# Moving the operands of TensorE's products to 0 or 64 bytes modulo 128 in a fused four-layer graph kernel

## The chip, the core and the metric

The program runs on one core of one Trainium2 chip. The metric is the device time of one execution in microseconds (us). Engines are named as in the profile: PE is TensorE's matmul side, PEld its weight loads, DVE is VectorE, ACT is ScalarE, POOL is GpSimd, SP is SyncE, which issues all transfers.

## What is computed

The input is 32 graphs of 256 nodes with 256 features, `x`, and a 256 x 256 matrix `adj` for each. Four blocks follow one another, each with a residual and a layer norm:

```
x = layernorm(x + relu(concat(x, adj @ x / deg) @ W.T))
x = layernorm(x + GCN(x, adj))                # three layers, two with relu and bias
x = layernorm(x + attention(x, adj))          # 8 heads of 64: softmax(q k^T) mixed with adj and exp(-adj)
x = layernorm(x + softmax_n(sum_m(q k^T * adj)) * v)
```

## The kernel before

**Split products.** Most products are made from two parts of each operand: a high part in the type fp32r and a low part, the rest, also fp32r. `product` (L1515 and on) issues high x high, high x low and low x high into the same PSUM bank. ACT makes the high part while it copies (`copy`, L409), DVE the low part by a subtraction (`lo`, L881). The tiles with the names `..._h` and `..._l` hold them: the weights `w0`, `w123`, `wqkv`, `wout`, `w3`; the adjacency `adjT` (four graphs deep); and `fT`, `sup`, `hidT`, `x2T`, `qkT`, `oT`, `x3T`, which each graph writes anew. The attention's products of probabilities and values (`attend`, L1773) and the transpositions (`transpose_tiles`, L1537, against the unit matrix `ident`) are in plain fp32.

**The order of the work.** It is written out by hand for every engine. A slot of the loop `slot(s)` issues, on PE, 336 products that belong to five consecutive graphs (for instance `hidden` and `support` of graph s-2, `scores` and `values` of s-3, `probs_t` and `attend` of s-4, `tail_adj_k` of s-5). Each graph costs 180 fp32r products with a moving operand of 256 columns, 12 with 512 (`values`), 12 with 384 (`tail_project`), 48 with 64 rows and 256 columns that run two at a time (`scores`), 40 transpositions, 32 fp32 products in `attend` and 8 short ones in `tail_adj_k`. `first_graphs` and `last_graphs` fill and drain the pipeline. Engines are kept in step by semaphores; SP loads graph g when graph g-2 has released its buffers, and stores a result once `y_sb` is written.

In every product the second argument of `mm` is the stationary operand, which a weight load brings in while the product before is still streaming, and the third the moving one. In the profile's names the moving operand comes first after the arrow: `psum<-wout_h,oT_h` streams `wout_h` over the stationary `oT_h`.

**Where the tiles lie.** `sb` (L37 and on) allocates the tiles of SBUF in the order of the source, each start rounded up to 32 bytes. With `HALF = 16` elements of 4 bytes, `space_0` and `space_1` are 64 bytes in each partition and `space_2` is 32. All of a tile's rows and blocks that a product takes are at multiples of 256 bytes from its start, except in `qkT`, whose rows of `N + HALF` elements put k 1088 bytes (64 modulo 128) behind q. So an operand's start modulo 128 is that of its tile.

Of the kernel before, what the change touches and what calls it, by code (L numbers as in the profile page):

```python
# [13 lines left out]
def graph_blocks_kernel(nc, x_d, adj_d, nodemask, xT_d, adjT_d, w0_d, w123_d, L1_b1, L1_b2, L1_b3, wqkv_d, wout_d,  # L14
# [3 lines left out]
    P = 128  # L18
# [12 lines left out]
    HALF = 16  # L31
# [5 lines left out]
    with ctx:  # L37
        def sb(name, shape, dt=F32):
            return ctx.enter_context(nc.sbuf_tensor(name, shape, dt))
# [18 lines left out]
        eps = sb("eps", [P, NT])  # L58


        w0 = [sb(f"w0_{s}", [P, FT, 2 * F], F32R) for s in "hl"]
        w123 = [sb(f"w123_{s}", [P, 3, FT, F], F32R) for s in "hl"]
        wqkv = [sb(f"wqkv_{s}", [P, FT, 3, INNER], F32R) for s in "hl"]
# [35 lines left out]
        x2T = [sb(f"x2T_{s}", [P, FT, N], F32R) for s in "hl"]  # L99


        v_sb = sb("v_sb", [P, NT, INNER])
        w0_raw = v_sb
        qkT = [sb(f"qkT_{s}", [P, 2, 2, N + HALF], F32R)[:, :, :, 0:N] for s in "hl"]
# [2 lines left out]
        psum_exp = sb("psum_exp", [P, 2, 2, NT])  # L107
        rsum = sb("rsum", [P, 2, 2, NT])
        probT = work[:, 1].rearrange("p (a h j i) -> p a h j i", a=2, h=2, j=NT)
        sb("space_2", [P, HALF // 2])  # L110
        oT = [sb(f"oT_{s}", [P, PAIRS, N], F32R) for s in "hl"]
        x3_pre = sb("x3_pre", [P, NT, F])
        x3 = sb("x3", [P, NT, F])
# [2037 lines left out]
```

How the kernel before makes its waits and increments, by code:

```python
        def x3_done(eng, g):  # L239
            if g < ACT_X3:
                reuse(eng, act_x3, once(g))
            else:
                eng.wait_ge(dve_x[2], g - ACT_X3 + 1)
# [1 line left out]
        def y_done(eng, g):  # L245
            if g < ACT_Y:
                reuse(eng, act_y, once(g))
            else:
                eng.wait_ge(dve_y, g - ACT_Y + 1)
# [1 line left out]
        def reuse(eng, semaphore, n):  # L251
            if n > 0:
                eng.wait_ge(semaphore, n)
# [8 lines left out]
        @block.sync  # L263
# [68 lines left out]
            load_nodes(1)  # L332
            sp.dma_start(wqkv_raw[:, :, :], wqkv_d).then_inc(dma_wqkv, 16)
            sp.dma_start(wout_raw[:, :, :], wout_d).then_inc(dma_wout, 16)
            sp.dma_start(w3_raw[:, :, :], w3_d).then_inc(dma_w3, 16)
            for k in range(2, G + 6):
                if live(k):
                    load(k)
                if live(k - 6):
                    store(k - 6)
            for b in range(2):
                sp.wait_ge(dma_out[b], 16 * (G // 2))
# [1 line left out]
        @block.gpsimd  # L344
        def _(pool):
            nc.gpsimd.memset(one[:, :], 1.0)
            nc.gpsimd.memset(eps[:, :], LN_EPS)
            nc.gpsimd.memset(minus_half[:, :], -0.5).then_inc(pool_const, 1)
            nc.gpsimd.memset(ident[:, :], 0.0).then_inc(pool_ident, 1)
            pool.wait_ge(pool_ident, 1)
            nc.gpsimd.affine_select(out=ident[:, :], in_=ident[:, :], compare_op=ALU.not_equal, fill=1.0,
                                    base=0, pattern=[[-1, P]], channel_multiplier=1).then_inc(pool_ident, 1)
```

## Time and profile before

| | |
|---|---|
| median of the runs shown | 1286.66 us (1285.0, 1286.66, 1288.16) |
| the profiled execution | 1284.71 us |
| its span, first to last instruction | 1282.9 us |
| granted TensorE clock, mean | 0.999 |
| busy: PE, PEld, DVE, ACT, POOL | 98%, 90%, 91%, 75%, 14% of the span |
| instructions: PE, DVE, ACT, POOL | 10848, 3671, 2563, 383 |
| DMA | 49.01 MB, 11.6% of the 16 engines' time on the main queue |

The span is what the trace covers; the 1.8 us between it and the profiled execution's time lie around it. The duration of a product in the trace reaches from its start to its modelled end, and products overlap: what one costs in a run of them is the distance from one start to the next, which is read from the times of the timeline. A line of the timeline that merges several instructions has their common stretch as its duration.

### The profile page before, as it was taken

The numbers are of one execution on the slowest core, as the hardware profiler recorded it, in microseconds if no ns is written. First come the engines' busy times: TensorE is split into PE (matmuls) and PEld (weight loads), VectorE is DVE, ScalarE is ACT, GpSimd is POOL, SyncE is SP. The second block draws the span as 40 slices with busy tenths as digits, with TensorE's granted clock in tenths as the row PEclk, the third lists the DMA queues.
The fourth block names the chain that finished last, engine by engine and source line by source line (L and its number), as shares of the span: only waits on it lengthen the run. The fifth ranks groups of instructions, "written<-read, shape, count | busy, mean of one in ns | idle before, by whom it ended". The sixth has DMA issues, their size and how long they took to land. (4 is left out here: it accounts for less than half of the span.)

```text
span 1282.9 us, 30378 instructions
## 1 busy us (share of the span) xinstructions
PE 1262.4 (98%) x10848; PEld 1158.9 (90%) x10848; DVE 1163.1 (91%) x3671; ACT 964.2 (75%) x2563; POOL 177.3 (14%) x383
## 2 busy tenths in 40 slices
PE   7999999999999999999999999999999999999997
PEld 6898999999999999999999999999999999999985
DVE  6988999999999999999999999999999999998995
ACT  7677778778778778777787787787787787787773
POOL 0100111101111101111111111011111011111011
PEclk9999999999999999999999999999999999999999
DMA  6110111110111110111100111101111101110000
GB/s 229 35 35 2 35 43 43 44 43 1 43 44 43 43 31 15 43 44 43 43 20 25 44 43 43 43 5 40 44 43 43 43 1 43 44 43 9 9 10 25
DMA packets 34309, 49.01 MB, mean 38 GB/s; under 512 B 7921, under 2 KB 16881, under 8 KB 34161
## 3 DMA queue, kind: packets, MB, share of 16 engines
q1 hardware_dynamic: 34160, 47.08, 11.6%
q8 instruction: 88, 1.44, 0.5%
q14 instruction: 61, 0.49, 0.1%
HBM read 38.68 MB, written 8.39 MB: 37 GB/s over the span
## 5 line engine op out<-in xcount | busy, mean ns | idle before, releaser
L558 ACT ACTIVATE work<-work,shift 128x256 f32<-128x256 f32 x512 | 253.4, 499 | 4.9 <-DVE shift L1073 4.9
L1092 DVE SCALAR_TENSOR_TENSOR work<-work,rsum,extra 128x256 f32<-128x256 f32 x512 | 216.8, 475 | 1.0
L409 ACT ACTIVATE work<-psum 128x512 f32<-128x512 f32 x256 | 138.1, 595 | 73.5 <-PE psum L1537 69.6
L1073 DVE CUSTOM_DVE_ANT_0 work<-psum,minus_big 128x256 f32<-128x256 f32 x512 | 189.6, 417 | 3.3 <-PE psum L1731 2.8
L359 POOL TENSOR_TENSOR mv<-mv,eps 128x2 f32<-128x2 f32 x128 | 31.0, 242 | 1085.8 <-DVE mv L931 1085.8
L409 ACT ACTIVATE sup_h<-psum 128x512 fp32r<-128x512 f32 x124 | 73.3, 591 | 111.3 <-PE psum L1523 110.9
L1523 PE MATMUL psum<-x2T_h,wqkv_h 128*128 128x256 f32 x512 | 145.7, 285 | 0.0
L1523 PE MATMUL psum<-x2T_l,wqkv_h 128*128 128x256 f32 x512 | 142.6, 279 | 0.0
L1523 PE MATMUL psum<-x2T_h,wqkv_l 128*128 128x256 f32 x512 | 142.5, 278 | 0.0
L1537 PE MATMUL psum<-ident,work 128*128 128x128 f32 x1024 | 129.0, 274 | 0.0
L1773 PE MATMUL psum<-work,v_sb 128*64 128x256 f32 x1024 | 124.6, 386 | 0.0
L409 ACT ACTIVATE qkT_h<-psum 128x512 fp32r<-128x512 f32 x128 | 75.3, 589 | 55.2 <-PE psum L1523 54.9
L1537 PEld LDWEIGHTS psum<-ident,work 128*128 128x128 f32 x1024 | 113.0, 141 | 1.4 <-DVE work L1092 0.6
L362 POOL TENSOR_TENSOR rstd<-mv,minus_half 128x2 f32<-128x2 f32 x128 | 106.9, 835 | 10.0
L1773 PEld LDWEIGHTS psum<-work,v_sb 128*64 128x64 f32 x1024 | 67.9, 136 | 36.3 <-issue 0.4
L558 ACT ACTIVATION_READ_ACCUMULATOR work<-work,shift 128x1 f32 x512 | 97.9, 191 | 0.0
L1523 PEld LDWEIGHTS psum<-x2T_l,wqkv_h 128*128 128x128 f32 x512 | 96.8, 189 | 0.0
L1523 PEld LDWEIGHTS psum<-x2T_h,wqkv_h 128*128 128x128 f32 x512 | 96.3, 188 | 0.4 <-DVE x2T_l L881 0.2
L881 DVE TENSOR_TENSOR sup_l<-psum,sup_h 128x512 fp32r<-128x512 f32 x124 | 85.0, 685 | 12.6 <-ACT sup_h L409 12.6
L1523 PEld LDWEIGHTS psum<-x2T_h,wqkv_l 128*128 128x128 f32 x512 | 96.3, 188 | 0.0
L910 DVE BATCH_NORM_STATS2 bn<-x_pre 128x6 f32<-128x256 f32 x256 | 94.8, 413 | 0.3
L881 DVE TENSOR_TENSOR qkT_l<-psum,qkT_h 128x512 fp32r<-128x512 f32 x128 | 86.4, 677 | 3.0 <-ACT qkT_h L409 3.0
(186 smaller groups left out, 3788.8 us busy)
## 6 DMA issues: line engine op xcount, KB each, us to landing
xT_sb<-in_xT SPq DMA_DIRECT2D x32, 256.0 KB, 2.7
adjT_sb<-in_adjT SPq DMA_DIRECT2D x32, 256.0 KB, 3.0
adj_sb<-in_adj SPq DMA_DIRECT2D x32, 256.0 KB, 4.7
x_sb<-in_x SPq DMA_DIRECT2D x32, 256.0 KB, 4.9
out<-y_sb SPq DMA_DIRECT2D x32, 256.0 KB, 4.7
work<-in_wqkv SPq DMA_DIRECT2D x1, 1536.0 KB, 11.0
mask_row<-in_nodemask SPq DMA_DIRECT2D x32, 32.0 KB, 4.6
w_raw<-in_w SPq DMA_DIRECT2D x3, 256.0 KB, 5.9
```

The lines of the kernel that those rows point to most:

```text
L359: nc.gpsimd.tensor_tensor(mv[:, k, :, 1], mv[:, k, :, 1], eps[:, :], ALU.add) \
L362: nc.gpsimd.tensor_tensor(rstd[:, k], mv[:, k, :, 1], minus_half[:, :], ALU.pow) \
L409: return nc.scalar.activation(dst, src, ACT.Copy, scale=scale)
L558: last = nc.scalar.activation(prob[:, p % 2, i, h], prob[:, p % 2, i, h], ACT.Exp, bias=shift[:, p % 2, h, i:i + 1], scale=-1.0, accum_out ...
L881: return V_.tensor_tensor(dst, src, f32(hi_part), ALU.subtract)
L910: last = V_.bn_stats(out=bn[:, k, t], in_=src[:, t])
L1073: last = V_.tensor_tensor_reduce(out=prob[:, p % 2, i, h], in0=bank(SCORES[p] + h)[:, i * N:(i + 1) * N], in1=minus_big[:, g % 2, i], scal ...
L1092: last = V_.scalar_tensor_tensor(out=prob[:, p % 2, i, h], in0=prob[:, p % 2, i, h], scalar=rsum[:, p % 2, h, i:i + 1], in1=extra[:, g % 2 ...
L1523: last = mm(dst, left, right, start=opens and n == 0, stop=closes and n == len(steps) - 1)
L1537: last = nc.tensor.transpose(dst[:, r * N + t * P:r * N + (t + 1) * P], src[:, t, block_of(r)], ident[:, :])
L1773: last = mm(bank(PV[p])[h * D:(h + 1) * D, 0:N], v_sb[:, k, (2 * p + h) * D:(2 * p + h + 1) * D], probT[:, p % 2, h, k], start=k == 0, sto ...
```

## The change

Three spacers: `space_3` (32 bytes) is put ahead of the weights, `space_4` (64 bytes) ahead of `v_sb`, and `space_2`, ahead of `oT`, grows from 32 to 96 bytes. No instruction is added, removed or reordered.

```diff
@@ -58,6 +58,7 @@
         eps = sb("eps", [P, NT])
 
 
+        sb("space_3", [P, HALF // 2])
         w0 = [sb(f"w0_{s}", [P, FT, 2 * F], F32R) for s in "hl"]
...
@@ -99,6 +100,7 @@
         x2T = [sb(f"x2T_{s}", [P, FT, N], F32R) for s in "hl"]
 
 
+        sb("space_4", [P, HALF])
         v_sb = sb("v_sb", [P, NT, INNER])
...
@@ -107,7 +109,7 @@
         psum_exp = sb("psum_exp", [P, 2, 2, NT])
         rsum = sb("rsum", [P, 2, 2, NT])
         probT = work[:, 1].rearrange("p (a h j i) -> p a h j i", a=2, h=2, j=NT)
-        sb("space_2", [P, HALF // 2])
+        sb("space_2", [P, HALF + HALF // 2])
         oT = [sb(f"oT_{s}", [P, PAIRS, N], F32R) for s in "hl"]
```

Start of the tiles in bytes modulo 128, from the sizes in the source and their order:

| tiles | before | after |
|---|---|---|
| `work` (prob, probT) | 0 | 0 |
| `ident`, `one` | 64 | 64 |
| `w0`, `w123`, `wqkv`, `wout`, `w3`, `adjT` | 32 | 64 |
| `x_sb`, `adj_sb`, `xT_sb`, `adjT_sb`, `exp_adj`, `mask_all` | 32 | 64 |
| `fT`, `sup`, `hid`, `hidT`, `x1`, `x2`, `x2T` | 96 | 0 |
| `v_sb` | 96 | 64 |
| `qkT`: q, k | 96, 32 | 64, 0 |
| `oT`, `x3`, `x3T`, `qkv3`, `k3`, `gate_prob`, `minus_gate` | 96 | 0 |
| `x4_pre`, `y_sb` | 0 | 32 |

## Rows read from the trace of the kernel before

**Rows 1.** The page: busy time of each engine, and the granted clock in 40 slices.
```profile
PE 1262.4 (98%) x10848; PEld 1158.9 (90%) x10848; DVE 1163.1 (91%) x3671; ACT 964.2 (75%) x2563; POOL 177.3 (14%) x383
...
PEclk9999999999999999999999999999999999999999
```

**Rows 2.** Busy time by window: a thousand us, one slot, the end's wout run.
```profile
core 0: us, PE busy (x) PEld busy (x) DVE busy (x) ACT busy (x) POOL busy (x), PEclk, DMA share, GB/s
200.00:1200.00 1000.00, 1000.00 (x8648) 922.51 (x8647) 925.56 (x2934) 769.71 (x2055) 145.79 (x308) 1.00 0.12 35
593.22:632.05 38.83, 38.83 (x339) 35.81 (x337) 35.95 (x115) 29.94 (x81) 5.70 (x12) 1.00 0.12 36
1260.40:1262.40 2.00, 2.00 (x20) 2.00 (x19) 1.97 (x7) 0.56 (x2) 0.00 (x0) 1.00 0.00 0
```

**Rows 3.** PE's timeline, sixteen transpositions; then their group (mean ns of one).
```profile
616.76 1.91 PE L1537 MATMUL psum<-ident,work 128*128 128x128 f32 x16
...
L1537 PE MATMUL psum<-ident,work 128*128 128x128 f32 x1024 | 129.0, 274 | 0.0
```

**Rows 4.** PE's timeline: first of 24 wout products, and the product after the last.
```profile
629.33 0.28 PE L1523 MATMUL psum<-wout_h,oT_h 128*128 128x256 f32 x1
...
632.05 0.28 PE L1523 MATMUL psum<-w_h,hidT_h 128*128 128x256 f32 x1
```

**Rows 5.** PE's timeline: 12 products of x2T, 8 of sup, and what follows.
```profile
613.03 0.28 PE L1523 MATMUL psum<-x2T_h,wqkv_h 128*128 128x256 f32 x1
...
614.45 0.28 PE L1523 MATMUL psum<-sup_h,w_h 128*128 128x256 f32 x1
...
615.39 0.33 PE L1824 MATMUL psum<-k,adjT_h 128*128 128x128 f32 x2
```

**Rows 6.** PE's timeline: x2T and wqkv again, seven products; eight of fT follow.
```profile
624.33 0.28 PE L1523 MATMUL psum<-x2T_h,wqkv_l 128*128 128x256 f32 x1
...
625.12 0.28 PE L1523 MATMUL psum<-w_h,fT_h 128*128 128x256 f32 x1
...
626.03 0.28 PE L1523 MATMUL psum<-adjT_h,sup_h 128*128 128x256 f32 x1
```

**Rows 7.** PE's timeline: eight products of 384 columns, eight of 512, and what follows each.
```profile
609.54 0.33 PE L1523 MATMUL psum<-w_h,x3T_h 128*128 128x384 f32 x1
...
610.92 0.28 PE L1523 MATMUL psum<-adjT_h,fT_h 128*128 128x256 f32 x1
...
633.41 0.39 PE L1523 MATMUL psum<-wqkv_h,x2T_h 128*128 128x512 f32 x1
...
635.24 0.28 PE L1523 MATMUL psum<-sup_h,adjT_h 128*128 128x256 f32 x1
```

**Rows 8.** PEld's timeline: loads ahead of products of 128 and 64 columns.
```profile
615.27 0.30 PEld L1824 LDWEIGHTS psum<-k,adjT_h 128*128 128x128 f32 x2
...
616.17 0.54 PEld L1523 LDWEIGHTS psum<-sup_l,w_h 128*128 128x128 f32 x4
```

**Rows 9.** PE's timeline: groups of four score products.
```profile
643.34 0.39 PE L1731 MATMUL psum<-qkT_l,qkT_h 64*128 64x256 f32 x4
...
644.27 0.40 PE L1731 MATMUL psum<-qkT_h,qkT_l 64*128 64x256 f32 x4
```

**Rows 10.** PE's timeline near the end: 17 wout products of the last graph.
```profile
1260.45 0.28 PE L1523 MATMUL psum<-wout_h,oT_h 128*128 128x256 f32 x1
...
1262.38 0.28 PE L1523 MATMUL psum<-wout_h,oT_l 128*128 128x256 f32 x1
```

**Rows 11.** Groups by form: ACT copies, DVE operations and a transposition with other starts.
```profile
L409 ACT ACTIVATE work<-psum 128x512 f32<-128x512 f32 x256 | 138.1, 595 | 73.5 <-PE psum L1537 69.6
...
L409 ACT ACTIVATE sup_h<-psum 128x512 fp32r<-128x512 f32 x124 | 73.3, 591 | 111.3 <-PE psum L1523 110.9
...
L1002 DVE SCALAR_TENSOR_TENSOR x_pre<-psum,rdeg,self_part 128x256 f32<-128x256 f32 x64 | 28.0, 478 | 4.4 <-PE psum L1523 0.6
...
L1159 DVE SCALAR_TENSOR_TENSOR x_pre<-qkv,gate_col,x 128x256 f32<-128x256 f32 x64 | 27.9, 477 | 0.1
```

**Rows 12.** DMA issues: a load to 32 modulo 128, a store from 0.
```profile
adj_sb<-in_adj SPq DMA_DIRECT2D x32, 256.0 KB, 4.7
...
out<-y_sb SPq DMA_DIRECT2D x32, 256.0 KB, 4.7
```

## Prediction

> **What bounds the kernel now.** [...] Busy time alone can be deceptive, so the windows come next: from 200 to 1200 us PE has no idle time at all, and a slot of 38.83 us has 38.83 us of PE beside 35.95 of DVE and 29.94 of ACT [rows 2]. So the end is set by how fast PE gets through a fixed list of products, and the thing to read is the distance between the starts of neighbours in the timeline, not their duration.
>
> Sixteen transpositions take 1.91 us, the last one 274 ns of it, so 15 distances make 1.64 us: 109.1 ns each [rows 3]. [...]
> - 24 products of `wout` take 2.72 us, 113.3 ns each [rows 4];
> - 20 products of `x2T` and `sup` take 2.36 us, 118.0 ns each [rows 5];
> [...]
>
> [...] All these moving operands begin at 32 or 96 modulo 128, so every piece of 64 bytes, counted from the operand's start, lies across a boundary of 64. That is the pattern that the change could remove.
>
> The same pair of tiles shows both speeds: `x2T` over `wqkv` costs 118 ns in one place [rows 5] and 0.79 / 7 = 113 in another [rows 6]. So there are two states that a run of products falls into and keeps. Near the end, with ACT busy for 0.56 of 2 us, `wout` has 1.93 / 17 = 113.5 ns as in the middle [rows 2, 10]. The stall therefore does not need a busy ACT. I read it as PE's own two streams, the moving operand and the weight load.
>
> A slot's timeline, run by run in the way of rows 4 to 6, holds 107 of the 180 products of 256 columns near 118 ns and 73 near 113.3.
>
> **The change part by part.** It adds and removes no instruction; everything is in the addresses.
>
> *Loads.* Where products are short, the loads stand alone: eight in 616.17 - 615.27 = 0.90 us, 112.5 ns each [rows 8]. These are from `adjT`, at 32 modulo 128. I keep 112.5 ns as the floor of a product of 256 columns. If alignment helps the load too, the floor could fall to the 109.1 of rows 3, which adds 180 x 3.4 = 0.61 us a graph; if it does not, nothing. I take nothing.
>
> *The cycle for each 64 bytes.* If it goes, 256-column products gain at least 113.3 - 112.5 = 0.8 ns each, 180 x 0.8 = 0.14 us a graph; the 12 of 512 columns gain 13.1 ns each, 0.16 us; the 12 of 384 columns 10.1 ns each, 0.12 us. Sum 0.42 us a graph, 13 us for 32. All of it lies on PE and so on the path that sets the end.
>
> *The second state.* It costs 118 - 113.3 = 4.7 ns on 107 products, 0.50 us a graph. The scores cost (644.27 - 643.34) / 4 = 0.233 us for four, of which two run at a time, 116 ns a pair [rows 9]; 24 pairs down to 112.5 are 0.08 us. Together 0.58 us a graph, 19 us in all. Nothing in the trace tells whether the state needs the odd starts. The bounds: all of it goes, -19 us; it stays, 0; or it takes the 73 quick products as well, 73 x 4.7 = 0.34 us a graph, +11 us. I take 0, since the mutual distances, from which two streams would collide, are kept.
>
> *Everything that is not fp32r.* [...] An ACT copy takes 595 ns to `work` (0) and 591 to `sup_h` (96), and a DVE operation 477 ns to `x4_pre` (0) and 478 to `x1_pre` (96): these engines show no care for the start within 1% [rows 11]. The transfers to a start of 32 and from one of 0 both land after 4.7 us [rows 12], and SP's queue gets no new wait. Nothing here.
>
> *Whether PE's gain arrives.* DVE has 38.83 - 35.95 = 2.9 us a slot to spare and ACT more [rows 2]. A slot shorter by 0.4 us, or even by 1.0, leaves both under it. If the cover ran out, DVE's total of 1163.1 us [rows 1] would be the next floor. What is late next are operands that DVE makes just ahead of their product; I take no loss for them.
>
> **Sum.** 1284.7 - 13 = 1271 us against the profiled execution's own time. The median of the runs shown is 2 us above that execution, so 1273 in its terms.
>
> [...]
>
> **The rivals.**
>
> *Nothing changes.* [...] Time 1286.7. That the spacers don't do what they say belongs here, with little chance: the sizes and the rounding to 32 bytes leave no room for it.
>
> *The whole stall goes.* [...] 13 + 19 = 32 us off, 1254.7 in terms of the median. [...]
>
> *Slower: the second state becomes the rule.* [...] If all 73 quick products of a graph fall to 118 ns, 0.34 us a graph, 11 us: 1297.5. It decides from the point at which fewer than 34 of the 73 would stay quick while the wide products keep what they cost now: under that half the loss is over 5 us. For it: the state is entered and left without a change of tiles [rows 5, 6], so it hangs on something fine that the shift may touch. Against: the distances are kept.
>
> [...]
>
> **How the numbers follow.** The chances: 0.28 for the forecast (the cycle per 64 bytes goes, the states stay), 0.17 for the whole stall, 0.30 for nothing, 0.25 for slower. A measurement of this kernel can tell 0.3%, 3.9 us, from no change. Faster 0.45, same 0.30, slower 0.25. The forecast for the side that holds most is 1273; on that side alone the range is 1254 to 1282. For 8 in 10 it has to take in nothing and most of slower as well: 1254 to 1297.
>
> **What would show it.** In the profile after, the `wout` run of 24 should take 2.70 us (112.5 each) and not 2.72; more clearly, eight products of 512 columns should take 1.73 us for 1.83, and eight of 384 1.30 for 1.38. Runs near 118 ns in the same places say that the states stayed; `x2T` and `sup` at 118 where they were, `wout` at 118 where it was 113.3, say that they spread. A slot should be 38.4 us long for 38.83. ACT's and DVE's means of one should not move. Wrong would be the forecast if the wide products still take 1.83 and 1.38 us: then the cycle per 64 bytes has nothing to do with the start, whatever the total does.

## The result, and the profile after

The changed kernel takes 1289.03 us (median of 11), the kernel before 1285.04 (median of 11, those of the first table among them). The ratio is 1.0027, 95% interval 1.0019 to 1.0034: a loss that can be told from nothing, and just inside the 0.3% that I had called the same. I had forecast 1273 us and a gain.

The page of the changed kernel, busy time of each engine:
```profile
span 1287.2 us, 30378 instructions
...
PE 1267.2 (98%) x10848; PEld 1163.5 (90%) x10848; DVE 1163.4 (90%) x3671; ACT 964.3 (75%) x2563; POOL 177.1 (14%) x383
```
The span grew by 4.3 us and PE's busy time by 4.8; DVE and ACT are where they were [rows 1]. PE has no idle time here either (columns as in [rows 2]):
```profile
200.00:1200.00 1000.00, 1000.00 (x8615) 922.04 (x8614) 922.10 (x2922) 768.50 (x2053) 145.67 (x308) 1.00 0.12 35
```
8615 products got started in the thousand us, and 8648 before [rows 2]. So the products themselves became dearer. PE's timeline of the changed kernel shows where (start, stretch, engine, line, operation; all lines stand two lower in its source):
```profile
592.23 0.28 PE L1525 MATMUL psum<-wout_h,oT_h 128*128 128x256 f32 x1
...
595.06 0.28 PE L1525 MATMUL psum<-w_h,hidT_h 128*128 128x256 f32 x1
...
596.47 0.40 PE L1525 MATMUL psum<-wqkv_h,x2T_h 128*128 128x512 f32 x1
...
598.32 0.28 PE L1525 MATMUL psum<-sup_h,adjT_h 128*128 128x256 f32 x1
...
611.45 0.33 PE L1525 MATMUL psum<-w_h,x3T_h 128*128 128x384 f32 x1
...
612.84 0.28 PE L1525 MATMUL psum<-adjT_h,fT_h 128*128 128x256 f32 x1
...
614.95 0.28 PE L1525 MATMUL psum<-x2T_h,wqkv_h 128*128 128x256 f32 x1
...
616.33 0.28 PE L1525 MATMUL psum<-sup_h,w_h 128*128 128x256 f32 x1
...
617.24 0.33 PE L1826 MATMUL psum<-k,adjT_h 128*128 128x128 f32 x2
...
631.19 0.28 PE L1525 MATMUL psum<-wout_h,oT_h 128*128 128x256 f32 x1
```
Read run by run:

| run | before | after |
|---|---|---|
| 24 of `wout` over `oT` | 2.72 us [rows 4] | 2.83 us |
| 12 of `w123` over `hidT`, right behind | 1.36 us | 1.41 us |
| 8 of 512 columns | 1.83 us [rows 7] | 1.85 us |
| 8 of 384 columns | 1.38 us [rows 7] | 1.39 us |
| 12 of `x2T` and 8 of `sup` | 2.36 us [rows 5] | 2.29 us |

From one `wout` run to the next a slot now takes 631.19 - 592.23 = 38.96 us, 0.13 more than 38.83 [rows 2]. The rows of the table make 0.11 + 0.05 + 0.02 + 0.01 - 0.07 = 0.12 of it, and 32 x 0.13 is 4.2 us, the loss. `wout` moved from 113.3 to 2.83 / 24 = 117.9 ns a product, and `sup` from 117.5 to 0.91 / 8 = 113.8. Nothing new appears: operands at 0 and 64 modulo 128 run in the same two states, 113.3 and 118 ns, as operands at 32 and 96, and other runs are in them. A mean between the two, as the 115.5 ns of the `x2T` run, comes from a run with products in both: the means of its first five over 28 slots are 117 to 122 ns, those of the other seven 113.5 to 113.7.

### The profile page after: what moved, and what is told of

Same layout as the page of the kernel before. It is cut to its first block and busy times, and to the rows that moved or that the text cites. A ratio compares the mean times of both kernels' runs of the same rounds, so it can differ in the third digit from the quotient of the medians.

```text
span 1287.2 us, 30378 instructions
## 1 busy us (share of the span) xinstructions
PE 1267.2 (98%) x10848; PEld 1163.5 (90%) x10848; DVE 1163.4 (90%) x3671; ACT 964.3 (75%) x2563; POOL 177.1 (14%) x383
## 5 line engine op out<-in xcount | busy, mean ns | idle before, releaser
L1539 PE MATMUL psum<-ident,work 128*128 128x128 f32 x1024 | 129.0, 274 | 0.0
```

Source lines behind the costliest of these rows:

```text
L1539: last = nc.tensor.transpose(dst[:, r * N + t * P:r * N + (t + 1) * P], src[:, t, block_of(r)], ident[:, :])
```

## What decides the state: the experiments

Two things had moved at once. The table of starts gives them modulo 128, and there the distances are kept. In whole bytes they are not: the weights moved by 32 bytes, `oT` and `x3T` by 32 + 64 + 64 = 160, so `oT` lies 128 bytes further from `wout` than before. Theory A is the start itself, theory B the distance beyond 128: from the starts in whole bytes, `wout` (moving) minus `oT` (stationary) is 192 modulo 256 before and 64 after. Where a mean per product is given without a timeline, it is over the same run of products in some 20 slots, from the trace's start times.

**The first spacer alone.** Against the kernel before:
```diff
+        sb("space_3", [P, HALF // 2])
         w0 = [sb(f"w0_{s}", [P, FT, 2 * F], F32R) for s in "hl"]
```


> Only the 32-byte spacer ahead of the weights: every fp32r operand starts at 0 or 64 modulo 128 as in the changed kernel, but all exact distances between weights, adjT, fT, sup, oT, x3T are those of before (v_sb falls to 0, on probT's start). Theory A (the start itself, 0 or 64 for 32 or 96, makes the loss): the wout run of 24 takes 118 ns a product as after, total 1289 us, 1.003 of before. Theory B (oT moved by 128 bytes against the weights, and that exact distance decides in which of the two states the run falls): wout stays at 113.3 ns, total 1285 us, ratio 1.000. If v_sb on probT's start costs something, attend's pairs are longer than 216 ns.

Measured: 1286.9 us, ratio 1.0011 (1.0002 to 1.0021). Its timeline:
```profile
591.93 0.28 PE L1524 MATMUL psum<-wout_h,oT_h 128*128 128x256 f32 x1
...
594.65 0.28 PE L1524 MATMUL psum<-w_h,hidT_h 128*128 128x256 f32 x1
```
2.72 us for the 24: 113.3 ns a product, with all fp32r operands at 0 or 64. Theory A falls for `wout`. `attend` was not longer with `v_sb` on probT's start: 117.4 ns from product to product over its 16, as before, the gaps at its ends included. The small rest of about 1 us comes from other runs: `x2T` over `wqkv` in `qk(.., 2)` and `w0` over `fT` behind it were at 118 ns where before they were at 114 to 115, and `adjT` over `sup` behind these at 114 for 118. These three changed their state although every distance among the weights, `adjT`, `fT`, `sup` and `x2T` was kept: theory B, taken as a rule for each pair, doesn't explain them.

**128 bytes ahead of oT alone.** Against the kernel before:
```diff
-        sb("space_2", [P, HALF // 2])
+        sb("space_2", [P, 2 * HALF + HALF // 2])
```


> The kernel before with 128 more bytes ahead of oT: no start modulo 128 changes; oT, x3, x3T, k3 lie 128 bytes further from the weights, as in the changed kernel. Theory A: nothing changes, 1285 us, wout 113.3 ns a product. Theory B: wout falls to 118 ns, 36 products x 4.5 ns x 32 = +5 us, total 1289 to 1290.

Measured: 1288.59 us, ratio 1.0021 (1.0011 to 1.003). Its timeline:
```profile
592.77 0.28 PE L1523 MATMUL psum<-wout_h,oT_h 128*128 128x256 f32 x1
...
595.60 0.28 PE L1523 MATMUL psum<-w_h,hidT_h 128*128 128x256 f32 x1
```
2.83 us: the loss is there without a single start changed modulo 128. The run of `x2T` and `sup` is at 115.5 and 113.3 ns a product as in the changed kernel too, against 117.8 in both before. Theory B holds for `wout`. But `x2T`, `wqkv`, `sup` and `w123` were not moved at all here: the products ahead of these runs whose distance changed are those of `w3` over `x3T`, since `x3T` lies behind `oT` and moved with it. So a run's state can change with no tile of its own moved. And since `oT` moved together with all tiles behind it, this run does not say which of its neighbours `oT`'s distance counts to.

**128 bytes ahead of everything.** Against the kernel before:
```diff
+        sb("space_3", [P, 2 * HALF])
         w0 = [sb(f"w0_{s}", [P, FT, 2 * F], F32R) for s in "hl"]
```


> The kernel before with 128 bytes ahead of the weights: all tiles from the weights on move together, no start modulo 128 and no distance among them changes; only ident and work stay. Theory A and theory B both say 1285 us and the same runs at 113.3 and 118 ns. If runs change their state here too, it is the absolute address at a larger period, or the distance to ident and work, or chance.

Measured: 1285.92 us, ratio 0.9998 (0.9989 to 1.0008), all runs in the states of before but for a few slots of `aggregate`, whose mean went from 118.7 to 119.4 ns, and of `x2T` behind it, from 121.5 to 122.6. Here `oT` begins at the same place modulo 256 as in the kernel with 128 bytes ahead of `oT` alone, and `wout` is quick all the same: it is not `oT`'s own address that counts.

**The change without its first spacer.** Against the kernel before:
```diff
+        sb("space_4", [P, HALF])
         v_sb = sb("v_sb", [P, NT, INNER])
...
-        sb("space_2", [P, HALF // 2])
+        sb("space_2", [P, HALF + HALF // 2])
```


> The change without its first spacer: weights, adjT, fT, x2T stay at 32 and 96; v_sb and qkT move by 64 bytes, oT and what follows by 128. Theory A: 1285 us. Theory B: as the kernel with 128 more bytes ahead of oT, wout at 118 ns, 1289 to 1290 us; attend's pairs stay at 216 ns with v_sb at 32.

Measured: 1289.58 us, ratio 1.0029 (1.0018 to 1.004), `wout` at 117.8 ns. The first spacer is not needed for the loss. The three runs that changed with the first spacer alone (`x2T` over `wqkv` in `qk(.., 2)`, `w0` over `fT` and `adjT` over `sup` behind it) changed here in the same way, to 117.8, 118.2 and 113.9 ns, though neither they nor the tiles that they use were moved; in the changed kernel, with both edits, they are as before. What they answer to was not found.

**The period.** Against the kernel before, 256 bytes more:
```diff
-        sb("space_2", [P, HALF // 2])
+        sb("space_2", [P, 4 * HALF + HALF // 2])
```


> The kernel before with 256 more bytes ahead of oT, x3, x3T, k3. Theory B1 (the distance between moving and stationary start counts modulo 256; 128 more put wout in the slow state): back to before, wout 113.3 ns a product, 1285.5 us, ratio 1.000. Theory B2 (a longer period, or any move of oT upsets it): wout at 117.8 ns and 1288.5 us again.

Measured: 1285.31 us, ratio 1.0001 (0.9992 to 1.001). Its timeline:
```profile
591.50 0.28 PE L1523 MATMUL psum<-wout_h,oT_h 128*128 128x256 f32 x1
...
594.22 0.28 PE L1523 MATMUL psum<-w_h,hidT_h 128*128 128x256 f32 x1
```
2.72 us again. With 128 bytes more (2.83 us) the loss comes, with 256 it goes: in this step the distance counts modulo 256.

**What the spacers of before are worth.** 64 bytes more put `oT` at the weights' own start modulo 128, 32 bytes more between the two:
```diff
-        sb("space_2", [P, HALF // 2])
+        sb("space_2", [P, HALF + HALF // 2])
```


> The kernel before with 64 more bytes ahead of oT: oT and x3T start at 32 modulo 128, as the weights wout and w3 do, so the mutual distance is 0 where it was 64. Theory K (the distance modulo 128 that all these kernels keep is what holds the streams apart): wout is slower than both states, 120 to 135 ns a product, the kernel 1290 to 1300 us. Theory L (only the two states exist): wout 113.3 or 117.8 ns, 1285 to 1289 us.

```diff
-        sb("space_2", [P, HALF // 2])
+        sb("space_2", [P, HALF])
```


> The kernel before with 32 more bytes ahead of oT: oT and x3T start at 0 modulo 128 against the weights at 32, a mutual distance of 96 (or 32) in place of 64. Theory K: between the distances 64 and 0, wout 114 to 125 ns. Theory L: 113.3 or 117.8 ns, 1285 to 1289 us.

Measured: 1291.53 us, ratio 1.005 (1.0035 to 1.0065), and 1289.47 us, ratio 1.0035 (1.002 to 1.0049). The timeline of the first:
```profile
595.43 0.29 PE L1523 MATMUL psum<-wout_h,oT_h 128*128 128x256 f32 x1
...
598.29 0.28 PE L1523 MATMUL psum<-w_h,hidT_h 128*128 128x256 f32 x1
```
2.86 us is 119.2 ns a product; the second's run takes 2.82 us, 117.5. With no distance modulo 128 left, `wout` is hardly dearer than the 117.8 ns of its upper level; theory K had wanted 120 or more for it. Theory L, only the two states, doesn't hold either: the time of the first, 1291.53 us, is over its 1285 to 1289 (and inside theory K's 1290 to 1300), and in both kernels the distances from product to product in the `wout` run vary between 115 and 120 ns and, in the first, up to 124, where before they are 112 to 115. `adjT` over `fT`, behind the products of `x3T`, went from 117.7 to 116.1 and 113.8 ns without being moved. Eight products of 384 columns rose from 173.4 to 176.2 and 176.5 ns each.

**The middle tiles.** Against the kernel before:
```diff
-        sb("space_1", [P, HALF])
+        sb("space_1", [P, 3 * HALF])
...
-        sb("space_2", [P, HALF // 2])
+        sb("space_2", [P, 2 * HALF + HALF // 2])
```


> The kernel before with 128 more bytes ahead of fT, sup, hidT, x2T, v_sb, qkT and 128 more ahead of oT (256 in all): the distances of the middle tiles to the weights and adjT change by 128, those of oT to the weights by 256. Theory B1: wout stays at 113.3 ns; of the other runs those at 117.8 ns with adjT or w0 may turn to 113.3 and those of x2T over wqkv at 113.3 to 117.8; all together between 1276 (107 slow products of a graph turn quick) and 1296 us (all slow). Rival: the states of these runs are chance and don't follow the distance, 1285 to 1289 us with the same runs quick and slow.

Measured: 1286.07 us, ratio 1.0004 (0.9995 to 1.0014). Inside, much was exchanged: the 16 products of `w0` over `fT` ahead of `wout` went from 117.9 to 113.8 ns, `sup` over `adjT` in `gcn_out` from 117.4 to 114.3; `x2T` over `wqkv` in `qk(.., 2)` from 114.8 to 118.0, the 512-column products from 228.8 to 232.1. `wout` stayed quick. The states follow the layout, and the sum came out even.

**A rule, and a layout made by it.** The rule that I tried: a run is quick where the moving start minus the stationary one is 192 modulo 256. The evidence for it was thin. In the kernel before, most of the quick products are in runs at 192, but of the 108 products in such runs only 48 are quick; of the 72 in runs at 64, 20 are. Against the kernel before:
```diff
-        sb("space_0", [P, HALF])
+        sb("space_0", [P, 3 * HALF])
...
+        sb("space_5", [P, 2 * HALF])
         sup = [sb(f"sup_{s}", [P, NT, F], F32R) for s in "hl"]
...
+        sb("space_6", [P, 2 * HALF])
         hidT = [sb(f"hidT_{s}", [P, FT, N], F32R) for s in "hl"]
...
+        sb("space_7", [P, 2 * HALF])
         x2T = [sb(f"x2T_{s}", [P, FT, N], F32R) for s in "hl"]
```


> Theory B1 as a rule: a run is quick where the moving start minus the stationary start is 192 modulo 256 (the stationary start 64 ahead), slow where it is 64. Spacers of 128 bytes ahead of adjT (in space_0), sup, hidT and x2T bring w0 over fT, w123 over hidT, sup over adjT, sup over w123, adjT over fT and x2T over wqkv all to 192; only adjT over sup and wqkv over x2T stay or go to 64. No start modulo 128 changes. If the rule holds, some 80 of the 107 slow products of a graph turn quick, 80 x 4.5 ns x 32 = 11.5 us less: 1274 us. If the states pass on from run to run regardless (theory I, inheritance), between 1280 and 1288 us.

Measured: 1280.7 us, ratio 0.9954 (0.9935 to 0.9972): faster than both kernels, by half of what the rule forecast, and inside the range of its rival, that runs take over the state of the one ahead (1280 to 1288). Its page and its timeline:
```profile
span 1279.4 us, 30378 instructions
```
```profile
609.41 0.28 PE L1526 MATMUL psum<-adjT_h,fT_h 128*128 128x256 f32 x1
...
610.32 0.62 PE L1526 MATMUL psum<-adjT_h,fT_l 128*128 128x256 f32 x4
```
Eight of `adjT` over `fT` take 0.91 us, 113.8 ns a product. Run by run, with the distance modulo 256 and the mean ns per product over 27 slots, to the start of what follows:

| run, moving over stationary | before | this kernel |
|---|---|---|
| `wout` over `oT` | 192: 113.4 | 192: 113.3 |
| `w123` over `hidT`, behind `wout` | 64: 113.3 | 192: 113.3 |
| `sup` over `adjT`, `gcn_out` | 64: 117.4 | 192: 114.7 |
| `adjT` over `fT`, `mix` | 192: 117.7 | 192: 113.8 |
| `w0` over `fT`, 16 ahead of `wout` | 64: 117.9 | 192: 113.4 |
| `w0` over `fT`, first 8 of `support0` | 64: 113.7 | 192: 117.4 |
| `sup` over `w123`, 8 | 192: 117.8 | 192: 117.8 |
| `x2T` over `wqkv`, `qk(.., 1)` | 192: 117.8 | 192: 117.8 |

Of the rows that changed, two go with the rule (`gcn_out` and the 16 of `w0`). `adjT` over `fT` turned quick although its distance was 192 already, so that part of the gain is not the rule's doing; `sup` and `x2T` stayed slow at 192, and `w0` in `support0`'s first half turned slow there.

**The same with longer rows in qkT.**
```diff
-        qkT = [sb(f"qkT_{s}", [P, 2, 2, N + HALF], F32R)[:, :, :, 0:N] for s in "hl"]
+        qkT = [sb(f"qkT_{s}", [P, 2, 2, N + 3 * HALF], F32R)[:, :, :, 0:N] for s in "hl"]
```


> The same with qkT's rows 128 bytes longer, so that k begins 192 in place of 64 bytes behind q modulo 256. Theory B1: the scores, too, go to 113.3 ns a pair, up to 24 pairs x 3 ns x 32 = 2 us less than the kernel without it, 1272 us. Theory I: within 1.5 us of that kernel.

Measured: 1282.56 us, ratio 0.9966 (0.9955 to 0.9977). Both expectations missed: it is 1.9 us slower than the kernel without it, not 2 us faster and not within 1.5. The scores didn't gain (66.5 ns from product to product in `scores(.., 2)` and `scores(.., 3)`, 66.1 without), and `x2T` over `wqkv` in `qk(.., 0)` behind them lost (125.2 for 123.4), as did the products of 384 columns (175.1 for 173.0).

**Half of the rule.** Against the kernel before:
```diff
-        sb("space_1", [P, HALF])
+        sb("space_1", [P, 3 * HALF])
...
+        sb("space_7", [P, 2 * HALF])
         x2T = [sb(f"x2T_{s}", [P, FT, N], F32R) for s in "hl"]
```


> 128 more bytes ahead of fT and 128 ahead of x2T: fT, sup and hidT change their distance to weights and adjT by 128, x2T and oT keep theirs modulo 256. Theory B1: w0 over fT quick (16 products more), sup over adjT mostly quick (24), adjT over fT and sup slow: -40 x 4.5 x 32 = -5 us at most, 1280 to 1283 us. Theory I: 1284 to 1288 us.

Measured: 1293.12 us, ratio 1.0051 (1.0036 to 1.0067): the slowest of all, outside what either theory had forecast (1280 to 1283 and 1284 to 1288). Its timeline:
```profile
593.82 0.28 PE L1524 MATMUL psum<-wout_h,oT_h 128*128 128x256 f32 x1
...
596.65 0.28 PE L1524 MATMUL psum<-w_h,hidT_h 128*128 128x256 f32 x1
```
`wout` and `oT` have the distance at which they were quick in every run so far, 192, and take 2.83 us. The `w0` run ahead of them was slow (117.6), though at 192 as well. So the distance of the pair is not the whole of it, and the rule as I had it fails. That runs hand on their level is seen behind `wout`: `w123` over `hidT` is at 113.3 ns in each kernel in which `wout` is, and at 117.8 to 118.0 in each in which it isn't, whatever its own distance. What sets the level of one given run, out of its distance, the run ahead and the products that lead in, stays open.

**The change with the distance restored.** Against the changed kernel:
```diff
-        sb("space_2", [P, HALF + HALF // 2])
+        sb("space_2", [P, 3 * HALF + HALF // 2])
```


> The changed kernel with 128 more bytes ahead of oT, so that its distances to the weights are those of before modulo 256, with all starts at 0 or 64 as the change has them. Theory B1: wout is back at 113.3 ns, the loss is gone, 1285 to 1287 us, ratio 1.000 to 1.001. Theory A (the start itself): 1289 us still.

Measured: 1287.78 us, ratio 1.0007 (0.9998 to 1.0016). Its timeline:
```profile
592.65 0.28 PE L1525 MATMUL psum<-wout_h,oT_h 128*128 128x256 f32 x1
...
595.38 0.28 PE L1525 MATMUL psum<-w_h,hidT_h 128*128 128x256 f32 x1
```
2.73 us: with all starts at 0 or 64, `wout` is quick again. What is left, 0.0007 of the time and inside the noise, can be seen in two `x2T` runs (122.6 for 121.5 ns, 125.3 for 123.3) and in the products of 384 columns (176.6 for 173.3). This kernel can't be told from the one before.

## Why the prediction was wrong

**What bounds it** was read rightly: PE without idle time, and the two levels of 113.3 and 118 ns. Most of what the kernels differ by is a count of products at one level or the other; the wide products and, with `oT` 32 or 64 bytes further, `wout` itself also took times between and above the two.

**The cycle for each 64 bytes** is the step that failed, the whole of the forecast's -13 us. I had taken a part of what every product costs for the price of pieces that lie across a boundary of 64 bytes. That this part is a cycle, and the 13.1 and 10.1 ns that a wide product was to gain, were my estimate, counted from a rate that no run shows. What the runs show in its place: with the pieces on the boundaries, the first spacer's kernel and the changed one still have 113.3 ns in their quick runs; the wide products take 228.8 and 173.3 ns in the first, as before, and in the changed kernel 1.85 and 1.39 us where I had forecast 1.73 and 1.30. Nor did `wout` come down to the 112.5 ns of the loads: in no kernel is its mean under 113.3. What I had written would refute the forecast is what happened. No row held an fp32r product at another start, and yet I gave "nothing changes" only 0.30. Why the quick runs take 113.3 ns and not less stays open; that a start at an odd multiple of 32 causes it is excluded, since they take it at 0 and 64 too.

**The second state: 0** was mis-sized by not seeing where the distances change. The step "the mutual distances are kept" failed: they are kept modulo 128 only, and my table, made modulo 128, hid the 128 bytes between `wout` and `oT`. That is 36 products at 4.6 ns, 0.16 us a graph or +5 us, less 0.07 us a graph regained in the `x2T` and `sup` runs: +3, and with the wide products and smaller runs the measured 4. I had this direction as the slower rival (+11 us for all 73 quick products, 36 of them really fell), but with the new starts as its cause and the distances as kept. That PE's two streams stall one another was my reading, and no run shows it. The cause of the loss was the distance of `oT` and the tiles behind it to the rest: the loss came with no start changed modulo 128 and went with the distance restored.

**The rest held**: ACT (964.3 us busy for 964.2), DVE (1163.4 for 1163.1) and the transfers (a load of `adj_sb` lands after 4.6 us for 4.7) were unmoved. So were the transpositions (129.0 us busy for those of `work` in both kernels) and the fp32 products of `attend` (117.4 ns in both), also with `v_sb` on probT's start. The measured time lies inside the range, on the other side of no change than the forecast. That is no merit of the working: the range reached so far for the sake of the slower rival, and the cause that I had in mind for it, the new starts, is one that the runs refute.

## What to carry to other kernels

Where a kernel streams fp32r products back to back, read the distance from start to start run by run. Here the same operands, `x2T` over `wqkv`, took 113 ns in one place and 118 in another [rows 5, 6], and `wout` over `oT` 113.3 ns with `oT` where it was and 117.8 with `oT` 128 bytes further. The level went with the layout, and in one place with the run ahead: `w123` over `hidT` took 113.3 ns behind a `wout` run of 113.3, and 117.8 to 118.0 behind a slower one. For one step, `oT` against the rest, it was the distance modulo 256 bytes that counted (2.72 us for the `wout` run with 0 and 256 bytes more, 2.83 with 128). Elsewhere runs changed with no distance of their own changed (`x2T` over `wqkv` in `qk(.., 2)` from 114.7 to 117.8 ns with the first spacer alone), and what picks the level of a given run was not found. Whoever inserts a spacer in such a kernel should compare full addresses and not the remainders for which it was made, and should time each layout: by their distances, the layout of the rule and its half were forecast at 1274 and at 1280 to 1283 us, and took 1280.7 and 1293.12. A gain of half a percent (ratio 0.9954) was to be had here from four spacers of 128 bytes, and a loss of the same size (1.0051) from two.

## What was not expected of the hardware

- The fp32r products of 256 columns have two lasting levels in this kernel, 113.3 and 117.8 ns. In most runs there is little between them; with `oT` 32 or 64 bytes further its run was at neither (117.5 and 119.2 ns). From the trace's start times, the next load begins 3.37 ns after the product in `wout` runs at 113.3 ns (mean of 648 in the kernel before) and 2.49 ns after it in those at 117.8 (648 in the changed kernel). It is not the mark of the upper level everywhere: `adjT` over `fT` has 3.29 ns at 117.7 (mean of 336 in the kernel before), and so does `wout` itself in the slowest kernel, the half of the rule, with 3.34 ns at 117.8 (mean of 648). That slow run need not have the cause of the changed kernel's.
- 128 bytes more ahead of `oT` cost 0.2% of the kernel (ratio 1.0021), and 256 cost nothing (1.0001).
- Runs changed their level in a kernel in which neither their tiles nor the distances between them had been touched: `x2T` and `sup` with 128 bytes ahead of `oT`, from 117.8 to 115.5 and 113.3 ns.
- Equal starts modulo 128 (64 bytes more ahead of `oT`) cost `wout` only 119.2 ns a product, 5% over 113.3.
